# A graph layer whose last 16 of 49 neighbour classes are summed from gathered rows instead of dense tiles

## The reference

```
xn  = layernorm(x)
w   = sigmoid(relu(xn[dst] @ W1 + b1) @ W2 + b2)
gnn = segment_sum(xn[dst] * w, src) / segment_sum(w, src)
x   = x + gnn + mix(xn)                 # mix: linear attention over heads
x   = x + top2_of_6_experts(layernorm(x))
```

## Time and profile before

| | before |
|---|---|
| median of 3 runs | 1781.68 us (1774.37 to 1782.38) |
| the profiled execution, its own time | 1775.93 us |
| its span | 1773.8 us |
| mean granted TensorE clock | 0.931 |
| PE, DVE, ACT, POOL busy | 81%, 76%, 45%, 37% |

### The profile page before, as it was taken

The page is one execution under the profiler, slowest core; times in us unless marked ns, Lnnn a source line. Parts: engine busy times, 40 slices in busy tenths (PEclk is TensorE's granted clock), DMA queues, the critical chain, the costliest instruction groups (busy, mean ns, idle before and its releaser), DMA issues.

```text
span 1773.8 us, 40181 instructions
## 1 busy us (share of the span) xinstructions
PE 1438.8 (81%) x12059; PEld 1337.7 (75%) x12059; DVE 1339.3 (76%) x3949; ACT 806.8 (45%) x1983; POOL 655.2 (37%) x666
## 2 busy tenths in 40 slices
PE   0147788646389999999999999999999579999897
PEld 0136677545378988989888898988989579998786
DVE  8998878999957777777777777777777556666565
ACT  1123555345435444444444544444444245554443
POOL 1563567473311222222222222222222333338876
PEclk9767888777689999999999999999999889999999
DMA  7000000013351111010111101111011255433442
GB/s 184 9 1 0 1 1 1 1 62 119 106 165 37 36 45 39 33 48 33 47 36 40 41 33 48 36 39 42 33 51 33 85 163 144 127 112 109 121 119 77
DMA packets 68547, 108.68 MB, mean 61 GB/s; under 512 B 14306, under 2 KB 47849, under 8 KB 68231
## 3 DMA queue, kind: packets, MB, share of 16 engines
q1 hardware_dynamic: 50726, 57.78, 11.6%
q0 software_dynamic: 17760, 50.16, 8.2%
HBM read 52.41 MB, written 57.47 MB: 62 GB/s over the span
## 4 chain that ended last, share of the span: by engine, by line
PE 63%; issue 12%; DVE 12%; POOL 5%; DMA 3%; ACT 3%; DVEq 1%; another core or an unknown queue 1%; SPq 1%; POOLq 0%; ACTq 0%
PE turned L1388 18%; PE front L1388 16%; PE turned L1370 10%; DVE sort_mem L1688 8%; PE turned L1529 4%; PE front L1549 4%; PE front L1529 4%; POOL acc_mem L769 4%; ACT a_ring L1126 2%; PE turned L1522 1%; PE front L1417 1%; PE front L1410 1%; DVE sort_mem L1696 1%; DMA gath_mem<-in_dst 1%
## 5 line engine op out<-in xcount | busy, mean ns | idle before, releaser
L1796 DVE TENSOR_TENSOR sort_mem<-lane_bf,sort_mem 128x512 bf16<-128x512 bf16 x1372 | 498.2, 406 | 207.2 <-PE turned L1370 189.9
L1126 ACT ACTIVATE a_ring<-turned 128x512 fp32r<-128x512 f32 (+2 forms) x686 | 370.9, 545 | 462.5 <-PE turned L1370 447.4
L1388 PE MATMUL front<-y_all,a_ring 128*128 128x258 f32 x2352 | 376.0, 297 | 37.6 <-ACT a_ring L1126 37.6
L1388 PE MATMUL turned<-y_all,a_ring 128*128 128x258 f32 x2450 | 387.2, 296 | 10.8 <-ACT a_ring L1126 10.8
L1388 PEld LDWEIGHTS front<-y_all,a_ring 128*128 128x128 f32 x2352 | 305.9, 190 | 44.7 <-ACT a_ring L1126 44.4
L1688 DVE TENSOR_TENSOR sort_mem<-sort_mem 128x320 f32<-128x320 f32 (+2 forms) x568 | 326.7, 637 | 3.0
L1388 PEld LDWEIGHTS turned<-y_all,a_ring 128*128 128x128 f32 x2450 | 317.4, 190 | 14.8 <-issue 11.6
L1370 PE MATMUL turned<-sort_mem 128*128 128x128 bf16 (+1 forms) x2695 | 258.7, 217 | 2.3 <-DVE sort_mem L1796 2.2
L1370 PEld LDWEIGHTS turned<-sort_mem 128*128 128x128 bf16 x2695 | 147.5, 98 | 36.8 <-DVE sort_mem L1796 3.1
L1327 PE MATMUL turned<-ident,sort_mem 128*128 128x128 f32 x286 | 58.7, 373 | 105.9 <-DVE sort_mem L1688 105.1
L2097 DVE COPY acc_mem<-feat_mem 128x1796 f32 x112 | 123.3, 1103 | 21.0 <-issue 21.0
(11 more groups left out here) (253 smaller groups left out, 2179.4 us busy)
## 6 DMA issues: line engine op xcount, KB each, us to landing
base<-token_lists SPq DMA_DIRECT2D x54, 258.0 KB
base<-token_lists SPq DMA_DIRECT2D x54, 130.0 KB
gated_rows<-tab_mem SPq DMA_DIRECT2D x49, 128.5 KB, 3.0
late_mem<-mixed_rows SPq DMA_DIRECT2D x49, 128.0 KB
mixed_rows<-base SPq DMA_DIRECT2D x12, 512.0 KB, 3.9
feat_mem<-in_L_ffn_expert_w SPq DMA_DIRECT2D x18, 256.0 KB, 5.9
base<-in_x SPq DMA_DIRECT2D x1, 3136.0 KB
base<-in_x SPq DMA_DIRECT2D x1, 2352.0 KB
```

The costliest lines, as they stand in the source:

```text
L1126: nc.scalar.activation(a_ring[:, k % 2, :, :].rearrange("p s n -> p (s n)")[:, 0:width], ps_a[k % 2][:, 0:width], ACT.Copy).then_inc(S["a_ ...
L1388: last = nc.tensor.matmul(ps_agg[odd], a_ring[:, k % 2, n, :], y_part(t, part), start=(t == 0 and part == 0), stop=(t == BLOCKS - 1 and pa ...
L1796: nc.vector.tensor_tensor(hot[:, k % 2, 0:pairs, 0:lanes, :], lane_bf[:, 0:lanes, :].unsqueeze(1).broadcast_to([P, pairs, lanes, 2]), edge ...
```

## The change

Only the first 33 classes stay dense: 39 slots, ten groups, 20 steps a round. The edges of the last 16 classes lie next to each other in the sorted keys. They are taken as one run of 1408 keys (11 chunks of 128, the surplus marked as ended). `store_parts` writes the 16 tiles of y in both parts to memory (`split_rows`). In each round POOL fetches for each chunk 128 rows of 516 numbers with one indirect transfer (`fetch_rows`) into the place of y tiles 33 to 43, each chunk's place once; DVE computes the row numbers (`place_rows`) from the keys that SP loads (`load_keys`) and writes four one-hot masks in fp32r (`mark_rows`); PE multiplies mask and rows (`add_chunk`, two products a chunk) into the same bank. The steps of all pieces are laid out anew. Where one index of a pair of rounds picked the ring side, `side` now does, because ten groups is no multiple that keeps the old form apart; semaphores that were free are shared; the counts in the second path are shifted.

```diff
-SLOTS = BLOCKS + SPLIT
+SPARSE = 16
+DENSE = BLOCKS - SPARSE
+SLOTS = DENSE + SPLIT
 SLOT_ROWS = 64
-assert SLOTS <= SLOT_ROWS
+assert BLOCKS + SPLIT <= SLOT_ROWS
+CHUNK_COUNT = 11
+CHUNK_RUN = 3
+CHUNK_RUNS = -(-CHUNK_COUNT // CHUNK_RUN)
...
-FIND_AT = (2, 14, 22, 24, 25)
-LANES_AT = 3
-TURN_AT = 9
-CHECK_AT = 12
+FIND_AT = (2, 10, 15, 17, 18)
+LANES_AT = 6
+TURN_AT = 10
+CHECK_AT = 13
+CHUNK_AT = {0: 0, 1: 1, 2: 2, 3: 3, 4: 4, 5: 5, 8: 6, 11: 7, 14: 8, 18: 9, 19: 10}
+FIRST_CHUNK_AT = {9 + c: c for c in range(CHUNK_COUNT)}
+ROWS_AT = 5
+ROW_MARKS_AT = (7, 9, 12, 14)
+FIRST_MARKS_AT = (1, 2, 3, 4)
...
-LEAD = dict(den=4, over_den=5, x2=6, stats=8, spread=10, norm=17, turn=18, turned=19, router=21, hidden=22, logits=24,
-            peak=28, exp=30, probs=37, top=40, top_exp=42, index=43, marks=44, share=46, rank=46, place=50)
+LEAD = dict(den=3, over_den=4, x2=5, stats=6, spread=8, norm=12, turn=13, turned=14, router=15, hidden=16, logits=18,
+            peak=20, exp=23, probs=26, top=28, top_exp=30, index=31, marks=31, share=33, rank=33, place=36)
...
+        def both_parts(t):
+            at = home_of_tile(t) * Y_TILE
+            return y_all[:, at:at + Y_TILE]
+
+        def row_part(c, k):
+            return y_part(DENSE + c, k)
...
+            def store_parts(t):
+                sp.wait_ge(S["split_ready"], t + 1)
+                sp.dma_start(split_rows[(t - DENSE) * P:(t - DENSE + 1) * P, :], both_parts(t).bitcast(F32)).then_inc(S["split_stored"], 16)
...
+            def load_keys(q):
+                sp.wait_ge(S["key_step"], KEY_STEPS + 3 * (q + 1))
+                if not isinstance(q, int) or q:
+                    sp.wait_ge(S["idx_staged"], 2 * q)
+                sp.nop().then_inc(S["slot_free"], 1)
+                for s in range(2):
+                    sp.load(start_regs[s:s + 1], run_start[s * SLOT_ROWS + SLOTS:s * SLOT_ROWS + SLOTS + 1, 0:1])
+                for s in range(2):
+                    at = sp.snap(start_regs[s], min_val=0, max_val=COLS * P - RUN_EDGES)
+                    sp.dma_start(run_keys[:, s, :], kept_flat[bass.ds(at, RUN_EDGES)].rearrange("(p c) -> p c", c=CHUNK_COUNT)).then_inc(S["kept_loaded"], 16)
...
+            def fetch_rows(i, odd, first, end):
+                pool.wait_ge(S["idx_staged"], i + 1)
+                for c in range(first, end):
+                    if not isinstance(i, int) or i:
+                        pool.wait_ge(S["sum_ps"], STEPS_PER_BLOCK + CHUNK_COUNT * (i - 1) + c + 1)
+                    pool.nop().then_inc(S["slot_free"], 1)
+                    nc.gpsimd.indirect_dma_start(
+                        out=both_parts(DENSE + c), out_offset=None, in_=split_rows,
+                        in_offset=bass.IndirectOffsetOnAxis(ap=row_at[odd][:, c:c + 1], axis=0)).then_inc(rows_in[c // CHUNK_RUN], 16)
+
             pool.wait_ge(S["kept_stored"], 32)
-            pool.wait_ge(S["key_at_ready"], 2)
+            pool.wait_ge(S["count_ready"], 5)
             gather_window(0)
             gather_window(1)
+            pool.wait_ge(S["split_stored"], 16 * SPARSE)
+            fetch_rows(0, 0, 0, CHUNK_COUNT)
             pool.wait_ge(S["mix_done"], MIX_BATCHES)
             nc.gpsimd.memset(before_bf, 1.0).then_inc(S["list_consts"], 1)
             nc.gpsimd.memset(ones_bf, 1.0).then_inc(S["list_consts"], 1)
@@ -866,13 +953,24 @@
             nc.gpsimd.affine_select(out=before_bf, in_=before_bf, compare_op=ALU.is_gt, fill=0.0, base=0,
                                     pattern=[[1, P]], channel_multiplier=-1).then_inc(S["list_consts"], 1)
             gather_window(2)
+            fetch_rows(1, 1, 0, 9)
+            fetch_rows(1, 1, 9, CHUNK_COUNT)
+            fetch_rows(2, 0, 0, 3)
             over_spread(0)
+            fetch_rows(2, 0, 3, 9)
             with nc.gpsimd.Fori(1, FULL // 2) as q:
+                fetch_rows(2 * q, 0, 9, CHUNK_COUNT)
+                fetch_rows(2 * q + 1, 1, 0, 3)
                 over_spread(2 * q - 1)
+                fetch_rows(2 * q + 1, 1, 3, 9)
+                gather_window(q + 2)
                 list_tokens(2 * q - 2, 2 * q - 2, 0)
-                gather_window(q + 2)
+                fetch_rows(2 * q + 1, 1, 9, CHUNK_COUNT)
+                fetch_rows(2 * q + 2, 0, 0, 3)
                 over_spread(2 * q)
+                fetch_rows(2 * q + 2, 0, 3, 9)
                 list_tokens(2 * q - 1, 2 * q - 1, 1)
+            fetch_rows(FULL, 0, 9, CHUNK_COUNT)
...
+            def add_chunk(i, odd, c, opens):
+                if c == 0 and (not isinstance(i, int) or i > 1):
+                    pe.wait_ge(S["sums_kept"], i - 1)
+                if c % CHUNK_RUN == 0:
+                    pe.wait_ge(S["onehot_ready"], CHUNK_RUNS * i + c // CHUNK_RUN + 1)
+                    pe.wait_ge(rows_in[c // CHUNK_RUN], 16 * chunks_in_run(c // CHUNK_RUN) * (i + 1))
+                for part in range(2):
+                    last = nc.tensor.matmul(ps_agg[odd], row_marks[odd][:, c, :], row_part(c, part), start=(opens and part == 0), stop=False)
+                last.then_inc(S["sum_ps"], 1)
...
+                    if j in chunk_at:
+                        add_chunk(i, odd, chunk_at[j], j == 0)
+                    aggregate(i, odd, j // 2, j % 2, 0 not in chunk_at)
...
             def find_edges(q, piece):
                 if piece == 0:
                     dve.wait_ge(S["window_in"], 32 * (q + 1))
+                    nc.vector.tensor_scalar(run_bound.bitcast(I32), thr_bits[:, bass.ds(q, 1)], KEY_BASE, None, ALU.bitwise_or).then_inc(S["key_step"], 1)
+                    dve.wait_ge(S["key_step"], KEY_STEPS + 3 * q + 1)
+                    nc.vector.tensor_scalar(found, window[:, 0:P], run_bound, None, ALU.is_lt, ALU.add,
+                                            accum_out=run_count).then_inc(S["key_step"], 1)
                     nc.vector.tensor_tensor(unkeyed.bitcast(I32), window.bitcast(I32), thr_bits[:, bass.ds(q, 1)].broadcast_to([P, 2 * P]),
                                             ALU.bitwise_xor).then_inc(S["unkeyed_ready"], 1)
+                    dve.wait_ge(S["key_step"], KEY_STEPS + 3 * q + 2)
+                    dve.nop().then_inc(S["slot_free"], 1)
+                    nc.vector.scalar_tensor_tensor(run_start, key_at[:, bass.ds(q, 1), 0], float(P), run_count, ALU.mult,
+                                                   ALU.add).then_inc(S["key_step"], 1)
...
+            def place_rows(i, odd):
+                keys_here = run_keys[:, odd, :]
+                dve.wait_ge(S["kept_loaded"], 32 * (i // 2 + 1) if isinstance(i, int) else 16 * (i - odd) + 32)
+                bits = keys_here.bitcast(I32)
+                nc.vector.tensor_scalar(row_block, bits, LANE_BITS, BLOCK_MASK << LANE_BITS, ALU.logical_shift_right, ALU.bitwise_and).then_inc(S["row_step"], 1)
+                nc.vector.tensor_scalar(row_from, bits, LANE_MASK, None, ALU.bitwise_and).then_inc(S["row_step"], 1)
+                nc.vector.tensor_scalar(row_into, bits, LANE_BITS, LANE_MASK, ALU.logical_shift_right, ALU.bitwise_and).then_inc(S["row_step"], 1)
+                ended = past[:, bass.ds(CHUNK_COUNT * i, CHUNK_COUNT)]
+                nc.vector.tensor_tensor(ended, keys_here, bound[:, bass.ds(i + 1, 1)].bitcast(F32).broadcast_to([P, CHUNK_COUNT]),
+                                        ALU.is_ge).then_inc(S["row_step"], 1)
+                dve.wait_ge(S["row_step"], ROW_STEPS * i + 1)
+                nc.vector.tensor_scalar(row_block, row_block, -float(DENSE * P), 0.0, ALU.add, ALU.max).then_inc(S["row_step"], 1)
+                dve.wait_ge(S["row_step"], ROW_STEPS * i + 4)
+                dve.nop().then_inc(S["slot_free"], 1)
+                nc.vector.scalar_tensor_tensor(row_lane, ended, float(P), row_into, ALU.mult, ALU.add).then_inc(S["row_step"], 1)
+                dve.wait_ge(S["row_step"], ROW_STEPS * i + 5)
+                nc.vector.tensor_tensor(row_at[odd], row_block, row_from, ALU.add).then_inc(S["idx_staged"], 1)
...
+            def mark_rows(i, odd, r):
+                if r == 0:
+                    dve.wait_ge(S["row_step"], ROW_STEPS * (i + 1))
+                    if not isinstance(i, int) or i > 1:
+                        dve.wait_ge(S["sum_ps"], STEPS_PER_BLOCK + CHUNK_COUNT * (i - 1))
+                of = slice(CHUNK_RUN * r, min(CHUNK_RUN * (r + 1), CHUNK_COUNT))
+                grid = [P, of.stop - of.start, P]
+                nc.vector.tensor_tensor(row_marks[odd][:, of, :], lane[:, :].unsqueeze(1).broadcast_to(grid),
+                                        row_lane[:, of].unsqueeze(2).broadcast_to(grid), ALU.is_equal).then_inc(S["onehot_ready"], 1)
...
+                    if not last and j == ROWS_AT:
+                        place_rows(i + 1, 1 - odd)
+                    if not last and j in ROW_MARKS_AT:
+                        if isinstance(i, int) and i == 0 and j == ROW_MARKS_AT[0]:
+                            dve.wait_ge(S["split_ready"], BLOCKS)
```

(40 more changed lines are left out.)

100 lines of the change are left out of this document (67 added, 33 removed).

## The result

The changed kernel took 2078.59 us (median of 4 runs, 2061.98 to 2093.29) against 1782.03 us for the kernel before: 1.163 times, 95% interval 1.158 to 1.168. That ratio leaves out the run of 2093.29, which counts as slow (1.5% above the fastest of the four). The sign was right; the size was not: 1913 us was predicted, and the range ended at 2025. The profiled execution took 2061.98 us, its span is 2060.2.

A forecast was written before the change was run, and what follows sets the result against it. POOL's queue was to become the bound in place of PE's: 21.2 us a round against 18.34, +131 us on 1775.9 gives 1907 profiled, 1913 us with the median's 5.8 above it; range 1860 to 2025.

The forecast's parts named there:

- What bounds the kernel before: In the rounds, 18.34 us each: PE's queue plus a small wait of 1.04 us for ACT's tiles.
- The price of a gather, 1.30 us on POOL whatever its bytes: POOL's queue: 1.30 us from gather to gather, eleven a round 14.30 us, in a POOL round of 21.2 us.
- Two small terms of the sum: POOL's round: +0.52 us for the longer gap behind over_spread, and 0.46 us for the edge of POOL's loop.
- Rival 1: POOL between two gathers: gathers cost the queue little, PE stays the bound, 1635 to 1685 us; chance 9%.
- DVE 14.6 us a round: DVE in the rounds: fewer marks, new masks and short operations sum to 14.6 us, hidden under PE's 15.1.
- PE 15.1 to 16.2 us a round: PE in the rounds: fewer products and builds cut 18.34 us to 16.2, or 15.1 if chunks fill the waits.
- So POOL's queue is full and the period is its sum: POOL's order in a round: its inputs come in time, it runs without a gap, 21.2 us a round.
- C: Follow-up theory: indirect transfers in POOL's queue delay PE's signals, which itself slows the loop build, copy, marks, product.
- A: Follow-up theory: POOL's queue is the bound as predicted; late signals only make it wait for chunks.
- The start of the rounds at no cost: Before the rounds: stores of split rows hidden, keys land about with the window, round 0 little delayed.
- Rival 3: POOL's transfers beside DVE copies: DVE slows them by 0.25 us each, round 24.7 us, time 2075; chance 10%.
- Rivals 4 and 5: In the rounds: PE loses its clock in waits, about 2325 us, 3%; the transfers themselves bind, some 5% more, 3%.

The follow-up runs named there:

- f32out: Changed kernel with the gathers' destination named as plain fp32 instead of fp32r, full result, chip 12: 1900.54 us, 1.1002 times the kernel before.
- nofetch: Changed kernel without its 539 gathers and PE's wait for them, gathered edges left out, chip 12: 1749.09 us, 1.0135 times the kernel before.
- before_wide5: Kernel before plus five unused gathers a round of 128 rows of 516 numbers, chip 12: 1730.68 us, 1.0014 times the kernel before.
- before_2: Kernel before, unchanged, run again for its trace on chip 0, where signals come late: one run, 1769.16 us.
- spare_late: Changed kernel with five other tiles for chunks 6 to 10 of odd rounds, chip 1 (late signals): 2106.48 us, 1.188 times the kernel before.
- nofetch_late: Changed kernel without its gathers, sums wrong for the last 16 blocks, chip 1 (late signals): 1751.50 us, 0.986 times the kernel before.
- after_3: Changed kernel, unchanged, run again on chip 1, where signals come late: 2053.35 us in one run.
- narrow_2: Changed kernel gathering 16 numbers a row instead of 516, chip 0 (late signals): 2048.36 us, 1.155 times the kernel before.
- half8: Half of the change: only the last 8 blocks fetched, six chunks a round, full result, chip 14: 1759.61 us, 1.015 times the kernel before.
- after_2: Changed kernel, unchanged, run again on chip 0, where signals come late: 2049.53 us, 1.153 times the kernel before.
- narrow: Changed kernel gathering and storing 16 numbers a row instead of 516, chip 12: 1894.09 us, 1.097 times the kernel before.

## Why the prediction failed, step by step

- **What bounds the kernel before** (PE's queue): right, as far as the runs go.
- **The price of a gather, 1.30 us on POOL whatever its bytes**: right. In f32out they start 1.25 to 1.46 us apart, most of them 1.25 to 1.31, rows of 64 bytes cost the same round (20.78 us), and the destination's type makes no difference. The sum of POOL's busy work, 15.3 us, was measured as 15.3; the whole queue, 21.2, as 20.8 where it runs full. Two small terms of the sum were 1.1 us too large together, and the others a little too small: the first gather behind over_spread starts 0.19 us after it and not some 0.82 (the lines at 916.49 and 917.54), and at the edge of POOL's loop, put at 0.46 us a round, the first gather comes 0.30 us after list_tokens, as between any two transfers in f32out. Two of the readings behind the price, 1.07 us for a transfer and 1.38 us from one to the next, are not in the earlier trace rows but of the round before it (715.97 and 717.35 in the trace of the kernel before); they change nothing. Rival 1, the cheap gathers, falls: 1.10 times before with all signals on time. The rule of the Trainium skill weighed there (DMA: Bandwidth & Descriptors, Anatomy of one DMA — SWDGE (gpsimd) path), by which many can be emitted before it shows, would have had that rival's time; the runs don't agree with it.
- **DVE 14.6 us a round**: 625.5/45.8 = 13.7. The masks took 0.42 us for 256 elements and 0.52 to 0.61 for 384, inside 0.42 to 0.63. Two of them in DVE's timeline of the changed kernel:

```profile
903.97 0.54 DVE L1929 TENSOR_TENSOR row_marks<-lane,sort_mem 128x384 fp32r<-128x384 f32 x1
...
934.80 0.42 DVE L1929 TENSOR_TENSOR row_marks<-lane,sort_mem 128x256 fp32r<-128x256 f32 x1
```

- **PE 15.1 to 16.2 us a round**: as busy time right (nofetch, clock 1.00: 610.5 us in 39.8 rounds, 15.3), as a gain that could be seen if POOL were free wrong. nofetch makes 17.57 us against 17.23 for before_wide5 on that chip, and 17.84 against 18.28 for before_2 on the other kind. The rival's 1635 to 1685 us was not to be had in this order.
- **"So POOL's queue is full and the period is its sum"**: this is the step that failed. It checked POOL's order against PE and DVE with every signal taken as sent when its instruction ends. On the punctual chips that holds, and the round is the forecast's within 0.4 us. The ratio of 1.100 there lies between the forecast's 1.074 and the upper end of its range (2025/1782 = 1.136), and 1900 us near 1913 is in part luck: the loss was 171 us where 131 was forecast, since the kernel before is faster there. On the chip that was timed, the eleven added transfers make half of PE's signals late; the loop of build, copy, marks and product stretches, POOL waits 3.6 us a round at its gathers, and the round is 24.04. C is shown in the kernel before; that it also makes the 3.2 us between 20.8 and 24.0 here is argued, from spare_late, where A fails. 46 x 2.84 = 131 us of the miss are this.
- **The start of the rounds at no cost**: mis-sized. The first copy of the front bank came 23.5 us later than before. The gathers themselves cost the start 11 us with all signals on time (540.6 in nofetch, 551.9 in f32out, chip 12) and 18.5 us with late ones (537.8 in nofetch_late, 556.3 in after_3, chip 1); so about half of the 23.5 us is the wait for the first rows, which was put at next to nothing.
- **Rival 3** (24.7 us a round) came near the number by another road: not the gathers got slow (mean 0.996 us), the signals did. Rivals 4 and 5 didn't decide: the clock fell to 0.89, with PE waiting a good part of each round, and PE's busy time grew to 17.9 us, still well under 24.0; narrow_2 took away nearly all of the gathers' bytes with no gain.

The trace of before held the sign, had it been asked: in 108 of 285 cases a PE signal given within 1 us of a transfer's start on POOL came late, in 0 of 859 with none in 2 us. With about three transfers a round the kernel before is some 1 us a round longer there (18.28 in before_2; on the punctual chips it has no trace of its own, and with five more transfers it takes 17.23 in before_wide5). A forecast would have had to ask what fourteen do.

Left open: why chips differ in this, what it is in an indirect transfer that holds PE's signals up, why an equal share of late signals costs one kernel more than another, and how half8 would do on a late chip. No version that computes the full result beat the kernel before; the only gain seen is nofetch_late's 1.4% (interval 0.7 to 2.1%), without the fetched rows.

## What to carry to other kernels

Price an indirect transfer on POOL at about 1.3 us of its queue, whatever the bytes, and add up the queue before you move work there: eleven a round were too many even on the best chip. Then look at the signals of the bound engine: if its consumers start late, together, and beside such transfers, added transfers may be paid for a second time in a loop that seems to have nothing to do with POOL (0.5 us a round for six in one kernel, 2.9 for five in another). Removing work from the bound engine is worth only what the next wait leaves: here 2 to 3 us of PE's work bought nothing on the punctual chips even with the gathers gone, and 0.4 us a round on the late kind.

## Not expected of the hardware

- Semaphore events of PE came often some us after the end of their instruction (a tenth over 3.0 us in the changed kernel), all but one (in after_2) given within 2 us of an indirect transfer's start on POOL, on chips 0 and 1 and that of the result; on chips 12 and 14 at most 1.1% were over 0.5 us late (narrow).
- The same kernel before took 1775 to 1777 us on the one kind of chip and 1727 to 1729 on the other, 18.28 us a round in before_2 and, with five unused gathers more, 17.23 in before_wide5; the new kernel was 1.15 to 1.16 times before on the one, and f32out 1.10 on the other.
- The number of transfers counts, not their size: 64-byte and 2064-byte rows gave 23.94 and 23.93 us a round on chip 0, 20.78 and 20.80 on chip 12.
